# 1024x1024 layers as seven block products for two tiles, with weight sums made on the chip and read from DRAM

## What is computed

```python
h = gelu(x @ fc1_w.T + fc1_b)                      # 256 -> 1024          (part two)
y = concat(h @ fc2_w.T + fc2_b, h @ We.T + be)     # 1024 -> 192 shared + 64 of the expert of this sequence
h = silu(y @ w1.T * s1) * (y @ w2.T * s2)          # 256 -> 1024          (part three)
h = gelu(h @ h1.T * t1)                            # 1024 -> 1024, weights are -1, 0, 1
h = gelu(h @ h2.T * t2)                            # 1024 -> 1024, the same
out = x + h @ w3.T * s3                            # 1024 -> 256
```

## Time and profile before

| | |
|---|---|
| median of 3 runs | 1229.43 us (1228.52 to 1230.08) |
| the profiled execution: its time, its span | 1229.19 us, 1227.5 us |
| granted TensorE clock, mean | 0.992 of 2.4 GHz |
| busy: PE, PEld, DVE, ACT, POOL | 96%, 77%, 56%, 33%, 14% |
| part three, PE's first to last matmul | 578.57 to 1223.14 us, 2816 matmuls |
| DMA traffic | 70.78 MB, 58 GB/s over the span |

### The profile page before, as it was taken

The page is one execution under the profiler, slowest core; times in us unless marked ns, Lnnn a source line. Parts: engine busy times, 40 slices in busy tenths (PEclk is TensorE's granted clock), DMA queues, the critical chain, the costliest instruction groups (busy, mean ns, idle before and its releaser), DMA issues.

```text
span 1227.5 us, 19196 instructions
## 1 busy us (share of the span) xinstructions
PE 1182.3 (96%) x6404; PEld 943.3 (77%) x6434; DVE 692.0 (56%) x1264; ACT 400.5 (33%) x649; POOL 173.0 (14%) x235
## 2 busy tenths in 40 slices
PE   4899999999988899999999999999999999999998
PEld 3577777777756788887888888888888888888886
DVE  2867767677763887887635336335353263443532
ACT  1456565555643323323212213122122131221311
POOL 1243433334322131221000000000000000000000
PEclk9999999999997899999999999999999999999999
DMA  3343444444431222212101001010010010100100
GB/s 98 115 117 121 136 123 119 128 118 121 148 93 61 65 73 68 85 51 69 35 1 51 0 0 51 0 51 0 0 51 0 0 51 0 51 0 0 34 0 18
DMA packets 45418, 70.78 MB, mean 58 GB/s; under 512 B 12096, under 2 KB 26320, under 8 KB 45392
## 3 DMA queue, kind: packets, MB, share of 16 engines
q1 hardware_dynamic: 45392, 70.44, 18.8%
HBM read 57.32 MB, written 24.12 MB: 66 GB/s over the span
## 4 chain that ended last, share of the span: by engine, by line
PE 86%; DVE 7%; issue 2%; DMA 2%; SPq 1%; ACT 1%; POOL 0%; DVEq 0%; POOLq 0%; ACTq 0%
PE bank L1169 53%; PE bank L1126 5%; PE bank L955 3%; PE bank L1144 3%; PE bank L936 3%; PE bank L1137 3%; PE bank L1013 2%; DVE neg_max L640 2%; PE bank L976 2%; PE bank L918 2%; PE bank L902 2%; PE bank L939 1%; PE bank L891 1%; PE bank L876 1%; DVE g_lo L783 1%
## 5 line engine op out<-in xcount | busy, mean ns | idle before, releaser
L1169 PE MATMUL bank<-h_lo,ffn_w 128*128 128x512 f32 x1152 | 450.8, 391 | 0.0
L1169 PE MATMUL bank<-h_hi,ffn_w 128*128 128x512 f32 x1152 | 450.8, 391 | 0.0
L1169 PEld LDWEIGHTS bank<-h_hi,ffn_w 128*128 128x128 f32 x1152 | 216.4, 188 | 47.3
L1169 PEld LDWEIGHTS bank<-h_lo,ffn_w 128*128 128x128 f32 x1152 | 216.3, 188 | 47.3
L825 DVE CAST h_hi<-h_raw 128x512 fp32r<-128x512 f32 x192 | 82.1, 427 | 298.9 <-ACT h_raw L587 296.7
L587 ACT ACTIVATE h_raw<-bank,scales 128x512 f32<-128x512 f32 x128 | 87.2, 688 | 322.0 <-PE bank L1169 321.9
L640 DVE TENSOR_REDUCE neg_max<-bank 128x2 f32<-128x512 f32 (+1 forms) x192 | 126.1, 686 | 52.5 <-remote 42.5
L827 DVE TENSOR_TENSOR h_lo<-h_raw,h_hi 128x512 fp32r<-128x512 f32 x192 | 133.0, 693 | 6.6
L501 ACT ACTIVATE p<-bank 128x512 f32<-128x512 f32 x192 | 111.3, 599 | 69.6 <-PE bank L955 66.0
L955 PE MATMUL bank<-q_t,keys 128*128 128x512 f32 x192 | 95.5, 516 | 4.8 <-DMA q_t<-m_t 4.2
L1169 PE MATMUL bank<-tile_lo,ffn_w 128*128 128x512 f32 x256 | 100.2, 391 | 0.0
(11 more groups left out here) (110 smaller groups left out, 1502.4 us busy)
## 6 DMA issues: line engine op xcount, KB each, us to landing
ffn_scratch<-in_ffn_d SPq DMA_DIRECT2D x16, 704.0 KB, 4.5
ffn_w<-ffn_scratch SPq DMA_DIRECT2D x16, 704.0 KB, 4.5
xt<-in_x_t SPq DMA_DIRECT2D x16, 256.0 KB
xtok<-in_x_tok SPq DMA_DIRECT2D x16, 256.0 KB
resid<-in_x_t SPq DMA_DIRECT2D x16, 256.0 KB, 3.1
x_scratch<-x SPq DMA_DIRECT2D x16, 256.0 KB, 2.6
tile_in<-x_scratch SPq DMA_DIRECT2D x8, 512.0 KB, 4.1
exp_raw<-in_exp_w SPq DMA_DIRECT2D x16, 256.0 KB, 2.7
```

The costliest lines, as they stand in the source:

```text
L1169: last = mm(bank, w_at(at, k, width, m), v_at(v, k), start=k == 0 and i == 0, stop=k == tiles - 1 and i == 1)
```

## The change

Part three takes two tiles at a time (`PAIRS`, four of them). The two tiles of a pair are the two block columns of a 1024x1024 activation matrix, whose features are the two block rows; with the weight matrix in four 512x512 blocks A11, A12, A21, A22, each 1024x1024 layer becomes seven block products instead of eight, in the order P1 = A11·b11, P2 = A12·b21, P6 = S2·t2, P7 = S3·t3, P4 = A22·t4, P5 = S1·t1, P3 = S4·b22.

- Activation sums: t1 = b12 − b11 and t2 = b22 − t1 on DVE; t3 = b22 − b12 and t4 = b21 − t2 on GpSimd, four 128x512 instructions each. Each of the seven operands is rounded to `op_hi` by ACT (`high`) and its rest made by DVE (`low`), in a ring of three.
- Output sums: P2 is accumulated onto P1's banks after ACT copied P1 to `u2`; DVE makes u2 += P6, u3 = u2 + P7, c21 = u3 + P4, c22 = u3 + P5, and, P3 being accumulated onto P5's banks, c12 = u2 + P3. ACT's gelu then works in place in SBUF for c21, c22, c12.
- Weights: `ffn_w` keeps only w1, w2, w3. The hidden weights come in eight chunks of 1 MB (`load_chunk`, two DMAs) into one buffer `comb`; GpSimd makes S1 to S4 of each (`combine`, four dependent 128x512 instructions), ACT sums the low 16 bits of the words (`check_chunk`), and SP stores seven blocks, 1.8 MB, to `hid_scratch` (`store_chunk`). Chunk 0 is handled between parts one and two, chunk t+1 in tile t of part two. Part three streams half products of 512 KB from there through `w_ring`, seven deep (`load_w`); the first seven are issued ahead of the last tile of part two.
- `bits` and its DVE work are gone; ACT also checks `ffn_w` in six pieces of 1024 columns (`check_piece`).

```diff
@@ SP @@
+            def load_chunk(c):
+                if not is_first(c):
+                    sp.wait_ge(s["comb_stored"], 16 * c)
+                    sp.wait_ge(s["comb_checked"], c)
+                    settle(sp, "sp_settled")
...
+                sp.dma_start(comb[:, A11:A11 + 3, :], src[:, 0:3, :]).then_inc(s["comb_loaded"], 16)
+                sp.dma_start(comb[:, A21, :], src[:, 3, :]).then_inc(s["comb_loaded"], 16)
+            def store_chunk(layer, k, c):
+                sp.wait_ge(s["comb_made"], 4 * (c + 1))
+                sp.dma_start(hid_scratch[layer, :, :, bass.ds(k, 1), :].rearrange("s p a c -> p s (a c)"), comb[:, 0:STORED, :]).then_inc(s["comb_stored"], 16)
...
+            store_chunk(0, 0, 0)
+            load_chunk(1)
             sp.dma_start(fc2_raw[:, :, :], fc2_w).then_inc(s["fc2_loaded"], 16)
...
                 load_expert(t)
                 if more:
                     load_x(t + 1)
+                    store_chunk(layer, k, t + 1)
...
-            with sp.Fori(0, TILES - 1) as t:
-                cond2_tile(t, True)
-            cond2_tile(TILES - 1, False)
+            with sp.Fori(0, 3) as t:
+                cond2_tile(t, 0, t + 1, True)
+                load_chunk(t + 2)
+            with sp.Fori(3, TILES - 2) as t:
+                cond2_tile(t, 1, t - 3, True)
+                load_chunk(t + 2)
+            cond2_tile(TILES - 2, 1, KB - 1, True)
...
+            sp.wait_ge(s["comb_stored"], 16 * CHUNKS)
+            for j in range(W_RING):
+                load_w(0, j)
+            cond2_tile(TILES - 1, None, None, False)
@@ ACT, hidden_layer @@
+                for m in range(KB):
+                    high(pair, o + P3, m)
+                    act.wait_ge(s["c21_ready"], KB * run + m + 1)
+                    gelu("c21", 1, m, x_blk[:, at["c21"], m], "x21_ready")
+                for m in range(KB):
+                    high(pair, o + PRODUCTS, m)
+                    act.wait_ge(s["c22_ready"], KB * run + m + 1)
+                    gelu("c22", 1, m, x_blk[:, at["c22"], m], "x22_ready")
@@ DVE, hidden_layer @@
+                for m in range(KB):
+                    low(pair, o + P3, m)
+                    product_done(P4, m)
+                    dve.wait_ge(s["u3_ready"], KB * run + m + 1)
+                    dve.wait_ge(s["t4_ready"], KB * run + m + 1)
+                    nc.vector.tensor_tensor(x_blk[:, at["c21"], m], banks[4 + m][:, :], u3[:, m, :], ALU.add).then_inc(s["c21_ready"], 1)
+                for m in range(KB):
+                    low(pair, o + PRODUCTS, m)
+                    product_done(P5, m)
+                    nc.vector.tensor_tensor(x_blk[:, at["c22"], m], banks[m][:, :], u3[:, m, :], ALU.add).then_inc(s["c22_ready"], 1)
@@ PE, product @@
+                            elif i == P2:
+                                pe.wait_ge(s["p1_out"], KB * run + m + 1)
...
+                            elif i == P3:
+                                pe.wait_ge(s["c22_ready"], KB * run + m + 1)
```

More of the change, by code:

```diff
@@ L11 @@
 I32 = mybir.dt.int32
-U32 = mybir.dt.uint32
+U16 = mybir.dt.uint16
 ALU = mybir.AluOpType
@@ new lines, in load_resid2 @@
+            def load_resid2(pair):
+                if pair:
+                    sp.wait_ge(s["out_ready"], HEAD + 2 * KD * pair)
+                for half in range(2):
+                    at = (2 * pair + half) * TW
+                    sp.dma_start(resid2[:, half], x1_scratch[:, :, at:at + TW]).then_inc(s["resid2_loaded"], 16)
+            sp.wait_ge(s["comb_stored"], 16 * CHUNKS)
+            for j in range(W_RING):
+                load_w(0, j)
+            cond2_tile(TILES - 1, None, None, False)
@@ new lines, in _ @@
+            for pair in range(PAIRS):
+                for m in range(KH):
+                    silu(pair, 0, m)
+                    if m == 3:
+                        y_high(2 * pair + 1)
+                for m in range(KH):
+                    silu(pair, 1, m)
+                    if m:
+                        high(pair, (m - 1) // KB, (m - 1) % KB)
+                high(pair, 1, KB - 1)
+                hidden_layer(pair, 0)
+                hidden_layer(pair, 1)
+                for o in (2 * PRODUCTS + 2, 2 * PRODUCTS + 3):
+                    for k in range(KB):
+                        high(pair, o, k)
@@ L1155, in ffn, with read @@
             def ffn(dt):
+                def read(w):
+                    return w if dt is F32R else w.bitcast(dt)
                 def w_at(at, k, width, m):
-                    w = ffn_w[:, at + k * width + m * P:at + k * width + (m + 1) * P]
-                    return w if dt is F32R else w.bitcast(dt)
-                def v_at(v, k):
-                    return v[:, k, :] if dt is F32R else v[:, k, :].bitcast(dt)
-                def part(bank, at, width, m, hi, lo, tiles, k, ready):
-                    if ready is not None and m == 0:
-                        pe.wait_ge(s["c_ready"], ready + k + 1)
-                    for i, v in enumerate((hi, lo)):
-                        last = mm(bank, w_at(at, k, width, m), v_at(v, k), start=k == 0 and i == 0, stop=k == tiles - 1 and i == 1)
-                    if k == tiles - 1:
-                        last.then_inc(s["c_mm"], 1)
@@ new lines, in last_layer @@
+                def last_layer(pair, half):
+                    for n in range(KH):
+                        o = 2 * PRODUCTS + 2 * half + n // KB
+                        k = n if half == 0 else (n + KB) % KH
+                        pe.wait_ge(s["op_ready"], KB * (OPERANDS * pair + o) + n % KB + 1)
+                        for m in range(KD):
+                            for v in (op_hi, op_lo):
+                                last = mm(banks[4 + 2 * half + m][:, :], w_at(W3_AT, k, D, m), read(v[:, o % OP_RING, n % KB, :]),
+                                          start=n == 0 and v is op_hi, stop=n == KH - 1 and v is op_lo)
+                            if n == KH - 1:
+                                last.then_inc(s["out_mm"], 1)
+                            elif n == KB - 1 and m == KD - 1:
+                                last.then_inc(s["w3_part"], 1)
```

487 lines of the change are left out of this document (352 added, 135 removed).

## The result

Over the executions compared, the changed kernel took 1289.01 us (median of 4, 1287.53 to 1290.23) against 1228.97 us (median of 4, 1226.28 to 1230.08) for the kernel before: ratio 1.0491, 95% interval 1.047 to 1.0513. It is slower by 60 us. The forecast was 1280 us, with a range of 1250 to 1300.

The account below looks back on a forecast made before the run. PE, busy 96%, bounds the kernel, with an equally long part-two loop through SP and GpSimd. 1229.2 +1 (part one) +57 (part two) -12.1 (part three) +3 (clock) +2.4 (tail) = 1280.5; forecast 1280 us, range 1250 to 1300.

Parts of the forecast that it names:

- Part one: Before part two: first chunk's loads (two issues, 1.3 us), against a smaller weight copy, add 1 us.
- The first y store: Start of part two: fc2 load behind 1 MB of chunk, GpSimd's sums among DVE's splits; moves from 421.25 to 435.2.
- Gate 1: Part two, first end of GpSimd's expert split after the first y store: at 451.6, 15.5 us later than before.
- The gate period: Part two, between ends of GpSimd's expert splits: sums, store, chunk issues, expert loads, split; 28.5 us against 22.1.
- Gate 7: Part two's last tile: seven 512 KB loads ahead of the expert loads; gate 32.2 us later, today 23.4, so +9.
- The turn of the alternating stretch: Part three from c21 on: gelu, `high`, `low`, sum in turn between ACT and DVE, 2.55 us against PE's 1.83.
- forecast waits per pair: Part three, PE: 3.9 first layer, 3.7 second layer's t1 and t2, 3.6 its end; 46.5 us in all.
- the clock's 3: Part three: 3 us added for a lowered PE clock after one or other of the waits.
- The tail: End of kernel: last two output instructions wait until the half before them is stored; +2.4 us.
- Rival 1: Part two: sums and store take 6.3 us instead of 12.7, gates keep PE's pace; about 1224 us, chance 4%.
- Rival 2: Part three reaches its matmuls' time, turn under 1.9 us: 1231 us, halfway 1255; together 11%.
- Rival 3: Part three's waits halve PE's clock once or twice a layer: +12 to +25, 1292 to 1305 us; chance 14%.

Follow-up runs that it names:

- e10: e8 with chunk 0's loads issued late in part one instead of ahead of the first copy of w1 to w3; 1177.24 us, ratio 0.9572.
- e7: e5 with e2's edit and three seam edits (fc2 load and biases before chunk 0's store, chunk 0's sums later, two halves of `outs`); 1183.42 us.
- e1: The changed kernel with chunk loads, and part three's first seven weight loads, moved behind the next tile's expert loads on SP; 1255.04 us, ratio 1.0206.
- e11: The changed kernel with each chunk stored twice, first to a spare area nothing reads, waiting for its landing; 1333.66 us, ratio 1.0846.
- e2: The changed kernel with ACT issuing each `high` one ahead in a layer's last three block sums; 1232.66 us, ratio 1.003.
- e5: e1 with ACT's chunk check behind the tile's gelus, chunks stored one tile later, and the checks' fold after part two's last tile; 1245.03 us.
- e3: The changed kernel with GpSimd starting t3 only when all of t2 is complete; 1274.62 us, ratio 1.0375.
- e8: e7 with t3 and t4 made on DVE, GpSimd idle in part three; 1180.89 us, ratio 0.9609.

## Why the forecast was right, point by point

- **Part one, +1 forecast, 5.8 measured** (last x1 store at 396.49; the kernel before has it at 390.69). This term was sized too small. The chunk's loads stand ahead of the first copy of the feed-forward weights, and SP waits for that copy: its next load is issued at 44.82 and not 42.77. In e10, with those loads late, it goes at 41.11. And chunk 0's four sums fall beside DVE's split of the first tile, which takes 1.76 + 2.17 us for 0.68 + 1.23; in e7, with the sums later, it takes 0.68 and 1.23 again. These two are 4.1 us. The other 1.7 were not traced, and are within what this part varies by: in the nine traces that share its code, the last x1 store lies between 392.89 and 398.22. With the edit of e7 it lies at 392.41, with that of e10 besides at 389.95.
- **The first y store,** 435.2 forecast, 441.67 measured. The fc2 load landed at 413.54 and not 408.7, 4.8 later by part one's loss; by its issue behind 1 MB of chunk it took 6.84 us, where the forecast had 7.2. The other 1.7 came behind it, where the chain goes by DVE's splits beside GpSimd's work (1.65 for 0.69) and PE's 48 narrow matmuls, 7.6 us for 5.89. Gate 1 came at 458.09 and not 451.6.
- **The gate period,** 28.5 forecast, 28.0 to 28.1 measured, the last of the five 28.6. The mechanism was right, and that the number is so near is in part luck, since pieces were off one way and the other: the sums took 6.7 instead of 5.7 us (I took DVE to be idle then, but its split of the next tile of x falls there, below; chunk 0's four take 5.39 in e7's trace, where DVE is idle), the store 6.23 instead of 7.0, the chunk's issues 0.9 instead of 1.3, from there to the second expert load's issue 7.1 instead of 6.1, and the split 3.7 instead of 5.24, without DVE beside it. e1 and e11 show the mechanism from both sides: take the round trip out of the loop and it ends, double it and it is paid again.
- **Gate 7,** 32.2 forecast, 31.9 measured. PE's matmuls behind it took 7.74 us for 5.89, 1.9 at the lower clock and not 3. All told part three began at 638.4, 1.9 us behind the forecast's 636.5.
- **The turn of the alternating stretch,** 2.55 forecast, 2.60 measured; that it is an order and not a rate, e2 shows. The forecast waits per pair were 3.9 (first layer), 3.7 (t1, t2), 3.6 (end). From the second pair's matmul starts I read 3.9, 3.7 and 3.8. Missing in the forecast was 0.85 at P6 of the first layer, and that each wait costs about 0.1 us more at its restart (`op_hi` to `op_lo` 0.34 us apart instead of 0.23), thirteen times a pair. So a pair took 160.7 us and the first, with nearly 2 us of lowered clock at w3, 162.2: part three 643.6 us, where 635.5 with the clock's 3 was forecast. These 8 us are most of the miss of 9.
- **The tail,** 2.4 forecast, 1.5 measured (5.8 us behind the last matmul, and 4.4 before).
- **The rivals.** Rival 1 fell with the first gate period. Rival 2 fell too, but e2 shows what it was worth: 56 us, where the forecast had put it at 49. Rival 3, a clock halved in each layer, did not come: over the four windows of 160 to 170 us that hold part three the granted clock is 0.99 to 1.00. Nor does a wait settle it: PE waits alike ahead of w3 in every pair (two matmuls start 1.5 and 1.8 us apart), but the clock fell there in the first pair alone, in e5 in the first two, in e1 in none. What the forecast did not say is that a reordering of ACT alone would make rival 2 true: it took the turn for given, and the turn was the order's.

The Trainium skill (DMA: Bandwidth & Descriptors, Anatomy of one DMA) gives a fixed 2.0 us and 436 GB/s for GpSimd's path; for 1792 KB that makes 6.2 us, as an estimate from that page. The store, issued by SP, landed in 6.23. In e5, in another place of the queue, it took 8.1 to 8.8 us from the second chunk on.

GpSimd and DVE held each other up, and not every instruction alike. In e3, while GpSimd makes t4 (738.10 to 744.94), DVE's `low` (L1048, both operands in SBUF) is stretched and its sum for u2 (L1086, one operand in a bank) is not:

```profile
742.00 0.68 DVE L1086 TENSOR_TENSOR u<-bank,u 128x512 f32<-128x512 f32 x1
742.61 1.18 DVE L1048 TENSOR_TENSOR op_lo<-x_blk,op_hi 128x512 fp32r<-128x512 f32 x1
743.71 0.68 DVE L1086 TENSOR_TENSOR u<-bank,u 128x512 f32<-128x512 f32 x1
```

By the Trainium skill (SBUF — State Buffer, SBUF: two separate sides), a DVE instruction with two SBUF inputs and a GpSimd instruction that reads SBUF shut each other out of a shared pair of ports, for the whole of the one that starts first; the trace agrees as to which of these two is stretched. Two SBUF inputs are not the only case here: the cast of the next x tile, with one, takes 1.68 instead of 0.68 us beside GpSimd's sums (last section).

## What to carry to other kernels

A queue that runs in program order turns a wait for a landed transfer into a wait for everything behind it: put the round trip behind the loads that the next step needs, and count it once in each loop that goes through the queue. Where two engines hand pieces over in turn, let the first engine run one piece ahead; here turns 0.77 us longer than PE's, and what hung on them, were 53 of the 644 us of part three, by one engine's order alone. Fewer matmuls give their time back only if what was put in their place finds slack, so cost the places first and the saving last.

## What was not expected of the hardware

- ACT loads its table, 1.28 us, ahead of the first gelu, in most tiles of part two. The kernel before did so as well, in ACT's idle time; in e1 it stood on the path behind the check (3.29) and the piece (1.06), in the first two long tiles, which were 5 to 7 us longer. In the traces of e5 to e8 and e10, with the check behind the gelus, no tile behind the first has such a load; why was not looked into.
- The first two of GpSimd's four dependent sums take 1.69 and 2.14 us in each gate period, the last two 1.28 and 1.30. DVE's timeline shows why: its split of the next x tile, released by a load behind the expert loads, falls beside the first two.

```profile
541.03 1.68 DVE L949 CAST tile_hi<-tile_in 128x1024 fp32r<-128x1024 f32 x1 [4.80 <-DMA tile_in<-x_scratch]
542.74 2.18 DVE L951 TENSOR_TENSOR tile_lo<-tile_in,tile_hi 128x1024 fp32r<-128x1024 f32 x1
```

- A wait of PE costs some 0.1 us beyond its length at the restart: behind it the first two matmuls start 0.34 us apart, and not 0.23.
